# A graph layer on one core: x W1 once per node in a DRAM table, 1 KB gathered rows, and the edge's logit on the vector engine

## What is computed

```
theta   = x[dst] - x[src]
w       = sigmoid(relu(theta @ W1 + b1) @ W2 + b2)        # one number per edge
agg     = segment_sum(w * theta, dst);  indeg = number of edges of dst
out     = layernorm(x + agg + indeg * (x @ W4 + b4))
```

## Time and profile before

| | |
|---|---|
| runs | 5248.12, 5259.45, 5257.63 us; median 5257.63 us |
| profiled execution | span 5257.5 us from the first to the last instruction |
| batches | 806, so 5257.5 / 806 = 6.52 us each |
| busy | PE 4021.0 us (76%), POOL 3071.6 (58%), DVE 2289.7 (44%), ACT 1222.0 (23%) |
| DMA engines | 44 GB/s over the span |

### The profile page before, as it was taken

The page is one execution under the profiler, slowest core; times in us unless marked ns, Lnnn a source line. Parts: engine busy times, 40 slices in busy tenths (PEclk is TensorE's granted clock), DMA queues, the critical chain, the costliest instruction groups (busy, mean ns, idle before and its releaser), DMA issues.

```text
span 5257.5 us, 79790 instructions
## 1 busy us (share of the span) xinstructions
PE 4021.0 (76%) x23554; PEld 2973.8 (57%) x23956; DVE 2289.7 (44%) x9032; ACT 1222.0 (23%) x2536; POOL 3071.6 (58%) x3231
## 2 busy tenths in 40 slices
PE   6777877777778777777777777777777877777776
PEld 4555555555556555555555555555555555555555
DVE  3444444444444444444444444444444444444444
ACT  2222222222222222222222222222222222222222
POOL 5555555556555655655565555655555565655554
PEclk8888888888888888888888887888888888888888
DMA  1111111111111111111111111111111111111111
GB/s 45 44 44 44 45 44 45 44 44 45 43 45 44 45 44 43 45 45 45 43 45 44 43 43 43 45 44 44 44 44 43 44 45 44 45 44 45 45 43 34
DMA packets 187593, 230.45 MB, mean 44 GB/s; under 512 B 105912, under 2 KB 136012, under 8 KB 187572
## 3 DMA queue, kind: packets, MB, share of 16 engines
q0 software_dynamic: 103296, 211.41, 15.5%
q1 hardware_dynamic: 84276, 18.80, 1.7%
HBM read 222.36 MB, written 7.60 MB: 44 GB/s over the span
## 4 chain that ended last, share of the span: by engine, by line
PE 53%; another core or an unknown queue 29%; issue 10%; ACT 6%; DVE 1%; SPq 0%; ACTq 0%; DMA 0%; DVEq 0%
PE ps_hid L399 15%; PE ps_log L407 11%; PE ps_sum L421 10%; PE ps_hid L382 7%; PE ps_srcT L391 5%; ACT hidden L486 3%; PE ps_rel L371 3%; ACT srcT L480 3%; PE ps_win L435 1%; ACT wgt L493 1%; PE ps_sum L415 0%; PE ps_win L429 0%; DVE hot_en L593 0%; ACTq L83 0%
## 5 line engine op out<-in xcount | busy, mean ns | idle before, releaser
L357 POOL DMA_INDIRECT gath<-in_x,src_i x3224 | 3070.9, 953 | 2145.3 <-remote 890.9
L593 DVE SCALAR_TENSOR_TENSOR hot_en<-col_no,rel,wgt 128x128 f32<-128x128 f32 x3224 | 920.2, 347 | 2025.7 <-ACT wgt L493 1498.1
L399 PE MATMUL ps_hid<-srcT,neg_w 128*128 128x512 f32 x1612 | 1081.2, 760 | 663.6 <-ACT srcT L480 421.1
L407 PE MATMUL ps_log<-w,hidden 128*128 128x1 f32 x6448 | 861.0, 255 | 416.2 <-ACT hidden L486 400.9
L407 PEld LDWEIGHTS ps_log<-w,hidden 128*128 128x128 f32 x6448 | 865.4, 209 | 473.8 <-issue 357.2
L421 PE MATMUL ps_sum<-gath,hot_en 128*128 128x129 f32 x6448 | 1015.8, 307 | 0.0
L584 DVE TENSOR_SCALAR_CACHE_REDUCE hot_ne<-ps_rel,row_no 128x512 bf16<-128x512 f32 x806 | 604.4, 750 | 781.7 <-remote 402.3
L486 ACT ACTIVATE hidden<-ps_hid,b_col 128x512 f32<-128x512 f32 x806 | 553.8, 687 | 1564.7 <-PE ps_hid L399 1028.9
L421 PEld LDWEIGHTS ps_sum<-gath,hot_en 128*128 128x128 f32 x6448 | 897.9, 215 | 0.0
L480 ACT COPY srcT<-ps_srcT 128x512 f32<-128x512 f32 x806 | 471.0, 584 | 1568.1 <-remote 1051.8
L399 PEld LDWEIGHTS ps_hid<-srcT,neg_w 128*128 128x128 f32 x1612 | 303.4, 235 | 704.3 <-ACT srcT L480 442.2
(11 more groups left out here) (67 smaller groups left out, 1015.7 us busy)
## 6 DMA issues: line engine op xcount, KB each, us to landing
gath<-in_x,src_i POOLq DMA_INDIRECT x3224
window<-in_x SPq DMA_DIRECT2D x116, 64.0 KB
out<-yout SPq DMA_DIRECT2D x116, 64.0 KB
first_i<-in_dst SPq DMA_DIRECT2D x116, 0.5 KB
src_i<-in_src SPq DMA_DIRECT2D x115, 14.0 KB
dst_i<-in_dst SPq DMA_DIRECT2D x115, 14.0 KB
w<-in_L_gnn_W SPq DMA_DIRECT2D x2, 64.0 KB
b_rows<-in_L_gnn_b SPq DMA_DIRECT2D x1, 64.0 KB
```

The costliest lines, as they stand in the source:

```text
L357: nc.gpsimd.indirect_dma_start(gath[0:parts, t, 0:F], None, x, bass.IndirectOffsetOnAxis(ap=src_i[0:parts, k.parity, t:t + 1], axis=0))\
L399: nc.tensor.matmul(ps_hid[b][:, :], neg_w1[:, :], srcT[:, b, :], start=False, stop=True)\
L407: last = nc.tensor.matmul(ps_log[:, t:t + 1], hidden[:, b, t * P:(t + 1) * P], w2[:, :], start=True, stop=True)
L593: last = nc.vector.scalar_tensor_tensor(hot_en[:, b, t, :], col_no[:, :], rel[:, k.parity, e:e + 1], wgt[:, b, t:t + 1].to_broadcast([P, P ...
```

## The change

A table of 12,500 rows of 1 KB is made in DRAM at the start: x W1 in the first 512 B of a row, x in the second. ACT issues four DMAs that copy x into its half; SP loads all of x into SBUF, PE transposes and projects it in 25 groups of up to 512 nodes, ACT copies the transposes, DVE copies the products, SP stores them. POOL waits until all of the table has been stored.

After that, a gather fetches the table's rows, and `gath` holds two chunks. The hidden layer has the edges on the partitions: PE multiplies the one-hot matrix by the three bf16 parts of the window's x W1 + b1 (`own_side`, 12 products of 128x128 per batch), DVE subtracts the gathered x W1 (`difference`) and takes relu, times W2, summed along the row, in one instruction per tile (`logits`). The one-hot matrix `hot_ne` is made by ACT in two steps (`distance`, `one_hot`). ACT multiplies the gathered x by the weight (`scale_rows`), DVE makes `hot_en` without the weight, in one instruction per batch (`one_hot_rows`). The edge counts are summed by PE, as a column of ones in `scaled_x`. SP loads the next chunk's indices when the chunk before has been read by `difference` (`z_read`).

```diff
-GW = 144
+GW = 264
+ONE = 2 * F
+SW = F + 3
+COPIES = 4
...
+        table = nc.dram_tensor("table", (z.nodes, 2 * F), FP32, kind="Internal").ap()
...
-        gath = sb("gath", [P, K, GW])
+        gath = sb("gath", [P, 2, K, GW])
...
+        def table_sync(sp):
+            for n, (row, rows) in enumerate(z.loads):
...
+                        sp.dma_start(all_rows[:, lo:lo + rows // P, :],
+                                     x[row:row + rows, :].rearrange("(t p) f -> p t f", p=P)).then_inc(rows_in[n], 16)
...
+        def table_store(sp):
+            for g, (row, rows) in enumerate(z.groups):
+                sp.wait_ge(values_copied, g + 1)
...
+                    sp.dma_start(table[row:row + rows, 0:F].rearrange("(t p) f -> p t f", p=P),
+                                 all_rows[:, row // P:(row + rows) // P, :]).then_inc(table_out, 16)
...
+        def table_scalar(act):
+            each = z.nodes // COPIES
+            for n in range(COPIES):
+                act.dma_start(table[n * each:(n + 1) * each, F:2 * F], x[n * each:(n + 1) * each, :])\
+                    .then_inc(table_out, 16)
+            for g, (row, rows) in enumerate(z.groups):
+                act.wait_ge(all_xT_ready, g + 1)
+                wait(act, values_ready, g - 1)
+                nc.scalar.copy(all_xT[:, g % 2, 0:rows], ps_rel[g % 2][:, 0:rows]).then_inc(all_xT_copied, 1)
...
         def windows_gpsimd(pool):
             pool.wait_ge(const_done, 1)
+            pool.wait_ge(table_out, 16 * table_stores())
...
                     if not is_first(k):
-                        pool.wait_ge(summed, (k.c - 1) * NB + j + 1)
+                        wait(pool, scaled, (k.c - 1) * NB + j + 1)
...
-                            gath[0:parts, t, 0:F], None, x,
+                            gath[0:parts, k.parity, t, 0:2 * F], None, table,
...
+            def own_side(k, j):
+
+                b = pair(k, j)
+                wait(pe, z_read, k.c * NB + j - 1)
+                wait(pe, hot_ready, k.c * NB + j + 1)
+                for t in range(B):
+                    for m in range(3):
+                        last = nc.tensor.matmul(ps_z[b][:, t, :], hot_ne[:, b, t * P:(t + 1) * P],
+                                                part[:, k.parity, m, :], start=(m == 0), stop=(m == 2))
+                last.then_inc(z_ready, 1)
...
+                nc.scalar.activation(away[:, b, :], ps_rel[b][:, :], ACT.Abs, bias=neg_row_no[:, :])\
+                    .then_inc(away_ready, 1)
...
+                nc.scalar.activation(hot_ne[:, b, :], away[:, b, :], ACT.Relu, bias=ones_col[:, :], scale=-1.0)\
+                    .then_inc(hot_ready, 1)
...
+            def scale_rows(k, j):
+                b = pair(k, j)
+                wait(act, wgt_ready, k.c * NB + j + 1)
+                wait(act, summed, k.c * NB + j - 1)
+                for t in range(B):
+                    last = nc.scalar.activation(scaled_x[:, b, t, 0:F + 1],
+                                                gath[:, k.parity, j * B + t, F:ONE + 1],
+                                                ACT.Copy, scale=wgt[:, b, t:t + 1])
+                last.then_inc(scaled, 1)
...
+            act.sem_inc(scaled, NB)
...
+            def difference(k, j):
+                b = pair(k, j)
+                wait(dve, gathered[k.parity][j], 16 * B * k.nth)
+                wait(dve, z_ready, k.c * NB + j + 1)
+                wait(dve, logit_ready, k.c * NB + j - 1)
+                nc.vector.tensor_tensor(diff[:, b, :, :], ps_z[b][:, :, :], gath[:, k.parity, j * B:(j + 1) * B, 0:F],
+                                        ALU.subtract).then_inc(z_read, 1)
...
+                for t in range(B):
+                    last = nc.vector.scalar_tensor_tensor(diff[:, b, t, :], diff[:, b, t, :], 0.0, w2_rows[:, :],
+                                                          ALU.max, ALU.mult, accum_out=logit[:, b, t:t + 1])
+                last.then_inc(logit_ready, 1)
```

More of the change, by code:

```diff
@@ L49, in __init__ @@
         self.node_tiles = nodes // self.gp
+        self.groups = [(r, min(B * P, nodes - r)) for r in range(0, nodes, B * P)]
+        self.loads = [(r, min(2 * B * P, nodes - r)) for r in range(0, nodes, 2 * B * P)]
 B = 4
@@ L192, in build @@
         const_done = sem("const_done")
-        neg_ready = sem("neg_ready")
+        rows_in = [sem(f"rows_in{n}") for n in range(len(z.loads))]
+        all_xT_ready = sem("all_xT_ready")
+        all_xT_copied = sem("all_xT_copied")
+        values_ready = sem("values_ready")
+        values_copied = sem("values_copied")
+        table_out = sem("table_out")
         src_in = [sem(f"src_in{n}") for n in range(2)]
@@ L448, in body @@
                             wait(pe, parts_ready, k.c + 1)
-                        hidden_dst(k, s)
-                    if now:
-                        transpose_src(k, s)
-                    if s - 1 < batches and at(k, s - 1):
-                        logits(*at(k, s - 1))
+                        own_side(k, s)
                     if s == WIN_STEP:
```

246 lines of the change are left out of this document (134 added, 112 removed).

## The result

| | this kernel, us | kernel before, us | ratio, 95% interval |
|---|---|---|---|
| first session | 6560.77 (6557.65 to 6572.48, 4 runs) | 5254.94 (5248.12 to 5259.45, 4 runs) | 1.2485 [1.2466, 1.2505] |
| forecast | 4220 (4120 to 4560) | | 0.80 |

The change makes the kernel 25% slower on this chip, where 20% faster was forecast. The profiled execution has a span of 6559.8 us. Later sessions were on other chips, and that turned out to be part of the answer: on two of six chips the kernel before takes only 4100 us, and variants of the changed kernel take 4240 to 4320 us.

The account below looks back on a forecast made before the run. The prediction took PE's pace to bound the kernel before, and POOL's gathers to bound the changed one: 130 us table + 4062 gathers + 30 end = 4222, forecast 4220 us, 20% faster, range 4120 to 4560.

Parts of the forecast that it names:

- POOL is held back by PE's pace: Kernel before: PE, busy 76%, sets the pace at 6.52 us per batch; the gathers' 4040 us floor is hidden under it.
- a changing clock plus round trips through ACT: PE in the kernel before: explained a mean batch of 6.52 us against a 3.95 us step at full clock.
- the one on the ring and on POOL's waits: Changed loop: engines' ring closes in 5.3 us per two batches against POOL's 10, so their mutual waits fall beside the gathers.
- Both waits should pass at once: POOL's waits in the changed loop: 35 us of slack for scaled rows, some 30 us for the index load.
- 1.26 us per gather: POOL's pitch with 1 KB rows, taken as 1.260 us: 3224 gathers take 4062 us.
- Table: Start of the kernel: POOL waits for the whole table, 75 to 405 us, taken as 130.
- sizes: DVE's instructions in the changed loop: 2.88 to 3.22 us per batch, 3019 to at most 3293 us over the run.
- end: After the last gather: its landing, one batch through the engines and the final work, taken as 30 us.
- The lock: Rival, chance 0.04: DVE instructions with two SBUF inputs keep POOL from writing descriptors, 0.54 us more per gather, 5960 us.
- the bytes: Rival, chance 0.03: a gather's price follows its row's bytes, 2.21 us each, 7290 us.
- The ring: Rival, chance 0.14: compute engines' waits on each other become the bound, 5.6 us per batch, 4670 us; decides from 5.04.
- forecast mechanism: Changed kernel, chance 0.78: POOL's back-to-back gathers set the time and compute hides beside them, 4220 us.

Follow-up runs that it names:

- experiment 6: The kernel before with gathers for the first chunk only: 3329.4 us, beside 5260.71 us for the kernel before on the same held chip.
- experiment 3: Two variants of the changed kernel: gathers at most 4 batches ahead of ACT, or POOL loading the indices; 5664.72 and 5611.81 us held, 4240.2 and 4313.12 free.
- lead4: The changed kernel with POOL's gathers at most 4 batches ahead of ACT's scaling: 4240.2 us on a free chip, 5664.72 us on a held one.
- experiment 4: A separate kernel without the computation, 512 PE instructions beside each traffic kind: 561 to 607 us beside gathers on a held chip, 16 to 17 free.

## Why the prediction was wrong

- *What bounds the kernel before.* "POOL is held back by PE's pace" was half of it. PE's pace is 4.04 us per batch (experiment 6), not 6.52; the other 2.5 us were filled with "a changing clock plus round trips through ACT", without a row that added up to them. Nor did missing records hide a busy PE: with as many records, 23554, the run without gathers shows PE busy 98%, so most of the 24% beside the 76% was true idle time.
- *The step that failed* is the one on the ring and on POOL's waits: "so it has some 30 us. Both waits should pass at once." It set each engine's work of a batch beside the gathers as if the two had nothing in common. On a held chip gathers and compute get in each other's way: PE issues 2.1 products per us beside a burst and 5.2 after it. The price of the chunk shown above: 35.1 us of gathers, in which about three of seven batches get done (76 of 24 x 7 products and a few for the window), then 17.3 us from the last gather's end at 3311.7 to the last difference's at 3329.05, then 2.8 us over the index load to the next gather: 55.2 us for 35.3.
- *The change made this worse than before.* The wait that I took away had kept the bursts short; the second buffer freed POOL for 28 gathers in a row, and the index load then kept it still while the engines caught up. Of the 2340 us between forecast and measurement, taking away the index wait gave 900 back (experiment 3). The rest is about what lead4 takes longer on a held chip than on a free one, 5665 against 4240 us.
- *POOL.* 1.26 us per gather and the price of a 1 KB row were right: 960 ns and 1.25 us in a burst, 1.274 us over lead4 on a free chip. 3224 x 0.014 = 45 us is all that the term missed there.
- *Table, sizes, end.* First gather at 110.4 us (130), end 44 us (30). The last packet of ACT's copies of x ended at 94 us, so the copies did not share one engine, which would have taken 395 us. DVE was busy 2571.0 us (3019 to 3293 was too high): an instruction of `logits` and its read take 289 + 82 ns as reckoned, but they overlap, and the four of a batch start 0.21 us apart (3317.99 to 3318.62 us in the trace) and not 0.368.
- *The rivals.* The lock and the bytes are ruled out: the gather's median is 946 ns beside all of DVE's new work. The ring had the right symptom (POOL waiting) with the wrong price and sign; its condition, 5.04 us per batch, was met because the engines were held up and not by the work that I had summed, which takes 3.8 us without gathers.
- *On a free chip* the forecast mechanism holds, as variants at 4240 to 4320 us show, and the forecast time of 4220 us would have been near, with the account of the kernel before still wrong. The forecast "20% faster" would be wrong there too: by its 4100 us the kernel before is bound by the same gathers, and the table's 105 us come on top; lead4 is 3.4% slower than it.

## What to carry to other kernels

A wait that paces a producer can be worth its time: here POOL's wait for PE's sums kept its bursts at some 6 to 9 gathers, and the kernel lost less beside them than with 28 in a row. Before giving a producer more lead, look at what its instructions do to the others: compare the pace of an engine's group without waits (here 12 products) while the producer runs and while it stands still. When work per step (4 us) and time per step (6.5 us) differ, find the rows of the difference before building on it; "issue" between instructions of one group is such a row. Time a baseline on more than one chip: the change costs 25% on some chips, and its variants 3 to 5% on others.

## What the hardware showed

- On four of six numbered chips (and in the first session) a back-to-back stream of indirect DMAs on POOL lets through about one instruction per gather on each of PE, ACT and DVE, one in 1.40 us. It lasts 4.5 us beyond a burst of 28 and some 25 us beyond one of 560; on the other two chips the gathers cost PE 3%. Neither row size, nor the code's length, nor plain DMAs from POOL or SP matter. Why chips differ is open; nothing here could test it.
- In a long stream on a held chip POOL's own pace falls from 1.25 to 1.40 us per gather after some 170 gathers, also in 610 to 780 us of experiment 4, where no other engine works (123 gathers in 170 us).
- A gather of 128 rows took 940 ns at the least with rows of 64 B, 512 B and 1 KB alike.
